# Attention with one ring of three PSUM banks, experts with two rings of row ids and registers loaded ahead

## What is computed

```python
x = x + attention(layernorm(x))          # 2048 tokens, width 512, 16 heads of 32, causal
x = x + ffn(layernorm(x))
x = x + rwkv(layernorm(x))
x = x + ffn(layernorm(x))                # the same weights again

def attention(x):
    q, k, v = split_heads(x @ w_project.T)
    att = softmax(where(causal, -1e9, q @ k.T / sqrt(32)))
    return (att @ v) @ w_out.T

def ffn(x):                              # 32 experts of width 352, each token in 6 of them
    scores = sigmoid(x @ gate_w)
    weights, experts = top_6(scores, within the 2 best of 4 groups)   # weights normed to sum 1
    out = sum(weights[e] * (silu(x @ w_gate[e]) * (x @ w_up[e])) @ w_down[e] for e in experts)
    return out + shared_ffn(x)
```

## Time and profile before

| | us |
|---|---|
| median of 3 runs | 3597.74 |
| lowest and highest | 3592.21, 3600.39 |
| the profiled execution | 3592.62 |
| its span, first to last instruction | 3590.6 |
| outside the span | 2.0 |

### The profile page before, as it was taken

How to read it: one execution, slowest core, us unless ns; L and a number is a source line. 1 busy time by engine, 2 the same in 40 slices (tenths; PEclk the granted TensorE clock), 3 DMA queues, 4 the chain that set the end, 5 groups by cost and what they waited for, 6 DMA issues and landing times. The chain is left out here.

```text
span 3590.6 us, 61956 instructions
## 1 busy us (share of the span) xinstructions
PE 3245.0 (90%) x15898; PEld 2440.5 (68%) x15901; DVE 2055.7 (57%) x3335; ACT 1584.2 (44%) x2094; POOL 1021.0 (28%) x772
## 2 busy tenths in 40 slices
PE   7899999998899799999999968877997999999996
PEld 6644444444467588888888843335776888888885
DVE  5165655563376355555555558987644555555554
ACT  2224444444221155555555546633114555554553
POOL 0100000000111134444434423432113444444443
PEclk9979999999999899999999979998998999999998
DMA  5411111110220256666666540014005666666654
GB/s 176 129 36 37 37 37 37 37 37 25 97 78 13 89 155 152 172 152 164 158 169 150 130 133 12 29 66 161 26 18 183 176 169 156 172 153 161 151 130 108
DMA packets 112728, 383.44 MB, mean 107 GB/s; under 512 B 18464, under 2 KB 19232, under 8 KB 100640
## 3 DMA queue, kind: packets, MB, share of 16 engines
q1 hardware_dynamic: 60000, 254.22, 21.3%
q0 software_dynamic: 52608, 127.69, 18.7%
HBM read 281.42 MB, written 104.63 MB: 108 GB/s over the span
## 5 line engine op out<-in xcount | busy, mean ns | idle before, releaser
L1583 DVE TENSOR_TENSOR g_lo<-g_raw,g_hi x232 | 562.8, 2426 | 431.4 <-ACT g_hi L1528 387.1
L1483 POOL DMA_INDIRECT acc_rows<-g_y,g_ids x232 | 414.8, 1788 | 895.2 <-DMA acc_rows<-g_y,g_ids 358.3
L1528 ACT ACTIVATE g_hi<-g_raw x232 | 469.3, 2023 | 430.6 <-issue 321.4
L544 DVE TENSOR_REDUCE b_part_max<-b_p_rows 128x1 f32<-128x512 f32 (+3 forms) x640 | 373.7, 608 | 292.1 <-PE b_p_rows L605 150.9
L518 ACT ACTIVATE b_probs<-b_p_cols 128x1024 f32<-128x1024 f32 (+1 forms) x320 | 279.7, 896 | 372.5 <-PE b_p_cols L625 371.2
L1635 PE MATMUL g_p_gate<-g_hi,g_rows_hi 128*128 x928 | 326.3, 352 | 40.1 <-issue 30.0
L1474 POOL DMA_INDIRECT g_rows_in<-xn_rows,g_ids x240 | 332.1, 1384 | 89.0 <-issue 89.0
L602 PE MATMUL b_p_rows<-b_k_stack,b_q_stack 96*128 96x512 f32 (+3 forms) x640 | 272.1, 449 | 38.8 <-DMA b_k_stack<-qk_hi 18.6
L1635 PE MATMUL g_p_gate<-g_lo,g_rows_hi 128*128 x928 | 305.2, 329 | 0.0
L1635 PE MATMUL g_p_gate<-g_hi,g_rows_lo 128*128 x928 | 304.7, 328 | 0.0
L1635 PE MATMUL g_p_up<-g_hi,g_rows_hi 128*128 x928 | 298.5, 322 | 0.0
(11 more groups left out here) (316 smaller groups left out, 6318.5 us busy)
## 6 DMA issues: line engine op xcount, KB each, us to landing
g_raw<-in_expert_weights_dram SPq DMA_DIRECT2D x64, 2176.0 KB, 9.1
acc_rows<-f_acc SPq DMA_DIRECT2D x34, 256.0 KB, 2.0
qk_hi<-a_hi SPq DMA_DIRECT2D x32, 256.0 KB, 2.5
qk_lo<-a_lo SPq DMA_DIRECT2D x32, 256.0 KB, 2.9
b_q_stack<-qk_hi SPq DMA_DIRECT2D x32, 256.0 KB, 7.7
b_k_stack<-qk_hi SPq DMA_DIRECT2D x32, 256.0 KB, 8.4
xn_rows<-f_xn SPq DMA_DIRECT2D x8, 1024.0 KB, 4.7
a_x<-in_x_dram SPq DMA_DIRECT2D x4, 1024.0 KB, 5.8
```

Source lines behind the costliest of these rows:

```text
L544: v.tensor_reduce(part_max[:, h, t % BT, c:c + 1], p_rows[:, u % NROWB, 0:w], AX.X, ALU.max).then_inc(rows_free, 1)
L1483: pool.indirect_dma_start(out=acc_rows, out_offset=bass.IndirectOffsetOnAxis(ap=ids[:, i:i + 1].bitcast(U32), axis=0), in_=y[:, n, :], in_ ...
L1528: act.activation(hi[:, bass.ds(place, PIECE)], raw[:, bass.ds(source, PIECE)], ACT.Copy).then_inc(split_hi_ready, 1)
L1583: v.tensor_tensor(lo[:, bass.ds(place, PIECE)], raw[:, bass.ds(source, PIECE)], hi[:, bass.ds(place, PIECE)].bitcast(F32), ALU.subtract).t ...
```

## The change

**Attention.** `b_p_rows` and `b_p_turn` become one tensor `b_p_ring` of three banks. Rows, turned shifts and turned outputs take its banks in turn, in the order in which PE makes them; each waits (`wait_ring`) until what stood there three places earlier has been read: a row by DVE's reduction, a shift by ACT's copy, an output by `block_out`. PE's order changes too: two steps are made together.

```diff
-    NPROB, NCOL, NROWB = 4, 2, 2
+    NPROB, NCOL, NRING = 4, 2, 3
...
-                    u = m * HPAIR + h
-                    pe.wait_ge(rows_free, n * NSTEP * HPAIR + u + 1)
...
+                    for m in range(0, NSTEP, 2):
+                        rows_ahead(m)
                         scores(n, i, m)
...
+                        scores(n, i, m + 1)
+                        if m in shift_at and not skipped(n, "shift", m):
+                            j, ahead = shift_at[m]
+                            wait_ring(n, "shift", m)
+                            turn_shift(n + 1 if ahead else n, j, bank("shift", m))
+                        rows_ahead(m + 1)
+                        if m + 1 in turn_at and not skipped(n, "out", m + 1):
+                            j, behind = turn_at[m + 1]
+                            wait_ring(n, "out", m + 1)
+                            turn_out(n - 1 if behind else n, j, bank("out", m + 1))
+                        for before in (m - LAG, m - LAG + 1):
+                            if before >= 0:
+                                products(n, i, before)
```

In the first pair SP also waits for the first stack of queries and keys before it issues the loads of the second:

```diff
                         load_stacks(0, 0)
+                        sp.wait_ge(loaded[0], LOADED)
                         load_stacks(1, 1)
```

```diff
-                def next_ids(t, i):
-                    v.wait_ge(added, (t - 1) * 16)
-                    v.sem_inc(ids_free, 1)
-                    v.tensor_copy(ids[:, i:i + 1], disp.row_ids[:, bass.ds(t + AHEAD, 1)]).then_inc(ids_ready, 1)
+                def next_ids(t, i, o):
+                    v.tensor_copy(ids_in[:, i:i + 1], disp.row_ids[:, bass.ds(t + AHEAD, 1)]).then_inc(ids_in_ready, 1)
+                    v.wait_ge(y_free, t)
+                    v.sem_inc(ids_out_free, 1)
+                    v.tensor_copy(ids_out[:, o:o + 1], disp.row_ids[:, bass.ds(t, 1)]).then_inc(ids_out_ready, 1)
```

```diff
-                            silu(t, i)
-                            split_next(t)
+                            piece = next_piece(t)
+                            silu(t, i)
+                            split_next(t, *piece)
...
-                            up(t, i, where(t))
-                            down(t - 1, 1 - i, where(t - 1))
+                            up(t, i, here)
+                            after = where(t + 1) if q < PER_TURN - 1 else None
+                            down(t - 1, 1 - i, before)
+                            before, here = here, after
```

More of the change, by code:

```diff
@@ L418, in is_last, with skipped, bank @@
             return isinstance(n, int) and n == NPAIR - 1
+        def skipped(n, kind, m):
+            if kind == "out":
+                return m == NSTEP and not is_last(n) or m < NSTEP and turn_at[m][1] and is_first(n)
+            return is_last(n) and (m + LEAD >= NSTEP if kind == "row" else shift_at[m][1])
+        def bank(kind, m, x=0, filling=False):
+            return (fill_at if filling else pair_at)[kind, m, x] % NRING
         with nc.Block() as block:
@@ L511, in pair @@
                     if is_first(n):
-                        copy_shift(0, 0)
-                        copy_shift(0, 1)
+                        for j in range(2):
+                            copy_shift(0, j, bank("shift", last_step[j] + 1, filling=True))
                     for m in range(NSTEP):
@@ L569, in pair @@
                             for h in range(HPAIR):
-                                reduce_unit(0, m, h)
+                                reduce_unit(0, m, h, bank("row", m, h, filling=True))
                             if m in last_step:
@@ L576, in pair @@
                             for h in range(HPAIR):
[L577 removed]
+                                reduce_unit(n + 1 if ahead else n, (m + LEAD) % NSTEP, h, bank("row", m, h))
                             if m in max_at:
@@ new lines, in wait_filling, with wait_ring @@
+                def wait_filling(at):
+                    kind, m, x = fill_order[at]
+                    if kind == "row":
+                        pe.wait_ge(rows_free, m * HPAIR + x + 1)
+                    else:
+                        pe.wait_ge(shift_copied, x + 1)
+                def wait_ring(n, kind, m, x=0):
+                    at = pair_at[kind, m, x] - NRING
+                    while at >= 0 and skipped(n, *pair_order[at][:2]):
+                        at -= NRING
+                    if at >= 0:
+                        wait_released(n, *pair_order[at])
+                    elif is_first(n):
+                        wait_filling(max(f for f in range(len(fill_order)) if f % NRING == at % NRING))
+                    else:
+                        last = max(f for f in range(STRIDE) if f % NRING == at % NRING and f < len(pair_order) - 1)
+                        wait_released(n - 1, *pair_order[last])
@@ new lines, in pair, with rows_ahead @@
+                        for at, (kind, m, x) in enumerate(fill_order):
+                            if at >= NRING:
+                                wait_filling(at - NRING)
+                            if kind == "row":
+                                rows_unit(0, 0, m, x, at % NRING)
+                            else:
+                                turn_shift(0, x, at % NRING)
+                    def rows_ahead(m):
+                        ahead = m + LEAD >= NSTEP
+                        if ahead and is_last(n):
+                            return
+                        if m + LEAD == NSTEP:
+                            pe.wait_ge(loaded[1 - i], next_loads * LOADED)
+                        for h in range(HPAIR):
+                            wait_ring(n, "row", m, h)
+                            rows_unit(n + 1 if ahead else n, 1 - i if ahead else i, (m + LEAD) % NSTEP, h, bank("row", m, h))
```

180 lines of the change are left out of this document (90 added, 90 removed).

## The result

| | us |
|---|---|
| kernel before, median of 4 runs | 3596.23 (3592.21 to 3600.39) |
| changed kernel, median of 4 runs | 3627.59 (3622.21 to 3645.01) |
| ratio, 95% interval | 1.0096 (1.0065 to 1.0127) |
| the changed kernel's profiled execution | 3645.01, span 3643.3 |

The change makes the kernel slower by 1.0%, 31 us. It was forecast to be faster by 53 us.

What follows compares the result with a forecast made beforehand. PE bounds attention and experts. Attention -41, scatter waits -70, turn top +10, collisions +62, existing collisions -14 make -53: 3592.6 becomes 3539.6, plus 5.1 for the median 3545 us; range 3485 to 3640.

Steps and rivals of the forecast that it cites:

- Attention, -41: Attention: third bank -80, turned outputs in the ring +43, filling part -4, together -41 us; ends -105 and +20.
- The turned outputs: Attention: the third row behind an output waits until `block_out` has read it, 1.34 us at 32 outputs: +43 us.
- The third bank: Attention: a row waits for the reduction three places back, not two: -80 of 105.6 us of waits.
- Wait for scatters, -70: Experts: DVE's ids copies no longer wait for recent scatters, so PE's resulting waits go: -70 us, bounds -82 and 0.
- top of the turn, +10: Experts, start of a loop turn: PE loads two numbers instead of one, 38 turns: +10 us, between 0 and +24.
- A collision, 6.94 us: Experts: a gather's issue, held by `g_lo`, ends when a weight load starts; PE's wait and slow start cost 6.94 us.
- The number of collisions, 9: Experts, both stages: 9 gathers caught by a weight load, +62 us, less -14 for the two already there.
- count of 22 periods: Experts: SP's timeline has 22 load periods of about 21 us in two stages; at most every second one collides, 11.
- the slower rival: Experts: collisions in periods of four tiles too, POOL a whole tile late; with 26 collisions +66, 3664 us; chance 0.14.
- the sign: Whole kernel: the change was forecast to make it faster, at 0.70; same 0.12, slower 0.18.
- The delay itself: Experts: a caught gather lands 9.6 us behind the load, though round robin by packet should delay it little.

Runs made afterwards that it cites:

- load_in_two_parts: The changed kernel with an expert's weights loaded in two parts of 1.1 MB, the second one tile later, nothing left out: 3458.69 us, ratio 0.9623.

## Why the prediction was wrong

**Attention, -41: the number right, in part by luck.** The pairs came out 38 us shorter in the trace (675 to 637), 33 in the medians. The turned outputs came as worked out: 39.5 us in 30 waits of weight loads, 1.32 each, where +43 in 32 of 1.34 was forecast. The third bank took 55 us of the rows' wait and not 80. By these rows the two terms make -15 and not -37; what gave the other 23 us, the new order of two steps or something else, no run shows.

**Wait for scatters, -70, and top of the turn, +10: nearly right.** The two times were 121 us over free tiles, and are 212. Less the late gathers (next paragraph) that is 106 and 54: -52, where -60 was forecast. In it PE's waits for `g_hidden` fell by 34 us over both times and its gaps ahead of `up` inside a turn by 10; those at the top of a turn rose from 21 to 33, that is by 12. The kernels with loads in parts show the register loads alone: 11.1 us a time over free tiles against 0.1 with the registers back, 22 in all, within the bound of 24. They also show that the 12 us a stage which the prediction gave to the top of the turn before were not of the registers as such: with the experts of before and loads in parts, 1.5 and 1.1 us are all that is left over free tiles.

**A collision, 6.94 us: right.** Measured as in the earlier trace rows, from one turn of hidden to the next, the 23 tiles with a late gather take 6.9 us each over 6.68 (from 1.4 to 10.1): a wait of 4.2 and a slow start of 2.7. That is 158 us. The kernel load_in_two_parts, which differs in the loads alone, is 190 us shorter in the two times, so some 30 us more went with the long loads outside these tiles.

**The number of collisions, 9: this is the step that failed.** "A collision makes its period 27 us, after which the next gather is clear of `g_lo`; so at most every second one, 11". There were 23. What it described, a gather's own issue held by `g_lo` until the load starts, did occur 7 times. The other 16 came by a path that the sum had at nothing: the scatter ahead of the gather is held, and the gather leaves behind it, into the load's traffic. The loads' starts show two more faults. Periods of four tiles have them too: for 9 of the 23, four or more tiles began between the load and the one before it; the forecast's count of 22 periods left these out and gave them only to the slower rival. And a collision clears nothing: three late gathers stand behind loads at 1736, 1761 and 1787 us, one after the other. The reason is that I looked at the place of one gather within one period, and not at the chain that sets it. In the changed kernel scatter to scatter is 5.65 us free, 7.2 when its issue is held, 10.4 across a load and 12.3 with both (medians); a period of four tiles with one load is 10.3 + 3 x 5.65 = 27.25 even without holds, against 26.7 on PE. By numbers that stood in the earlier trace rows POOL's chain is longer than PE's work in either kind of period, so a gather queued in it falls back, in the 16 cases by more than a tile behind its ids, until a load catches it. PE's stall is then how the chain gets its time back. Before, the same time was paid by DVE's wait for scatters, which reached PE in pieces of some 0.7 us and without slow starts; with that wait put back 6 late gathers are left of 23. As I read it, the change did not remove a wait; it removed the cheap way of paying for it. Put into the sum, 23 collisions in the place of 9 give +14 x 6.94 = +97 and turn -53 into +44, where the trace has +52.7. That was the rival "slower: periods of four tiles too", which I gave 0.14; its condition, POOL a whole tile late, is what the 16 show, though by the held scatter and not by the gather's own issue.

The range, 3485 to 3640, holds the median of 3627.6; the sign did not come out.

**The delay itself.** The prediction took the 9.6 us behind a load from the row and weighed against it the Trainium skill, "DMA: Bandwidth & Descriptors", section "Queues, rings and completion order", by which the DMA engines go round robin between queues packet by packet. From that it worked out that a gather beside a load would be delayed little. All 23 late gathers ended 8.9 to 10.7 us behind a load, so the small delay did not come. The turns themselves the trace does show. Behind the load at 1402.01 POOL's queue moves no packet for 4 us; in the next 3, from 1406.01 to 1409.01, the two queues move about as many packets each:

```profile
q1 hardware_dynamic: 53, 0.92, 79.9%
q0 software_dynamic: 50, 0.22, 19.2%
```

Packet by packet the turns are equal, as that section of the Trainium skill says, as far as its packets are those that the trace counts. But a packet of the load has 17.4 KB and one of the gather 4.4, so POOL's queue gets a fifth of the bytes. Why it has no packet in the first 4 us no run shows.

## What to carry to other kernels

Where a wait is to be removed, add up the chain that it waits for, over a whole period and with the traffic it meets: here three scatters and one load are 21.6 us against 20.0 of PE, so the time that the wait stood for had to come back somewhere. Add the issues to it that another engine's operation can hold: a held scatter pushed 16 of the 23 late gathers. A small wait that comes often can be the throttle that keeps a large one away. And where small DMAs that an engine waits for share the DMA engines with a large one, cut the large one first: two parts of 1.1 MB for one of 2.2 were worth 113 us with the experts of before (3554.9 to 3441.7; 118 with each beside its own runs of before), in the kernel that is 4.3% faster than the one we started from. In all these kernels the second part was issued only when the first had landed, and it is not shown that two parts without a gap would do.

## What the runs showed of the hardware

- Small DMAs caught behind a DMA of 2.2 MB land about 10 us behind its issue. With two of 1.1 MB, the second issued when the first has landed, a scatter is followed by the next 7.4 us on: in the gap of 1.6 us between the parts the small DMAs move 0.42 MB.
- `g_lo`, a DVE operation with two SBUF inputs, holds an indirect DMA's issue on POOL for nearly its own length: it takes 2.42 us, and an issue that meets it 2.99 where a free one takes 1.01. With `g_lo` in two halves the same kernel is 79 us faster.
- After a wait of 5.34 us for a gather PE's granted clock is 0.50 for the next 3.65 us at least; the 23 late gathers cost PE 4.2 us of waiting and 2.7 of slow start each.
- Two register loads ahead of the first matmul of a turn cost PE 0.5 to 0.6 us each turn (17 to 18 us of the launch and 22 us of the two times, over 38 turns); one between `up` and `down` costs nothing that the trace shows.
